# Interaction scratch laid out by quad, x loaded by quad, the last stores dealt out anew

## What is computed

```python
combined = concatenate([dense[:, None, :], e], axis=1)              # (2048, 27, 128)
interactions = einsum('bfd,bgd->bfg', combined, combined)           # (2048, 27, 27)
z = concatenate([dense, interactions[:, iu, ju]], axis=1)           # iu, ju: f < g
h = relu(concatenate([z, dense], axis=1) @ W_top1 + b_top1)         # (2048, 512)
h = relu(h @ W_top2 + b_top2)                                       # (2048, 256)
y = h @ W_top3                                                      # (2048, 1)
```

## Time and profile before

| | |
|---|---|
| runs | 359.15, 359.31, 359.65 us |
| profiled execution | 359.83 us |
| its span | 358.0 us |
| TensorE products busy | 325.9 us |
| VectorE busy | 240.7 us |
| ACT busy | 183.7 us |
| GpSimd busy | 250.0 us |
| mean granted clock of TensorE | 0.986 |
| DMA packets under 512 B | 26790 of 48069 |

### The profile page before, as it was taken

One profiled execution on the slowest core, in us unless ns is written; L12 is line 12 of the kernel. 1 busy time (PEld: TensorE's weight loads), 2 busy tenths in 40 slices (PEclk: granted clock), 3 DMA queues, 4 the chain that ended last, 5 costly groups with the idle time before them and its releaser, 6 DMA issues.

```text
span 358.0 us, 10391 instructions
## 1 busy us (share of the span) xinstructions
PE 325.9 (91%) x4192; PEld 312.3 (87%) x4192; DVE 240.7 (67%) x721; ACT 183.7 (51%) x360; POOL 250.0 (70%) x264
## 2 busy tenths in 40 slices
PE   0558789999999999999999999999999999999576
PEld 0548679989999998999899999999899999998565
DVE  3889987996469762995389654986299556951012
ACT  1345555556633763457534664557445664366224
POOL 5777777777777777777777777777777777775020
PEclk9987999999999999999999999999999999999989
DMA  5999657664447434662457444653356344421230
GB/s 146 235 249 246 157 160 193 158 168 133 99 101 181 115 76 103 139 170 69 99 120 187 95 82 106 149 149 69 103 131 185 82 98 102 125 68 46 34 78 0
DMA packets 48069, 44.80 MB, mean 125 GB/s; under 512 B 26790, under 2 KB 42150, under 8 KB 48022
## 3 DMA queue, kind: packets, MB, share of 16 engines
q1 hardware_dynamic: 38448, 26.89, 31.8%
q0 software_dynamic: 8320, 16.87, 19.5%
q10 hardware_dynamic: 1254, 0.39, 0.6%
HBM read 39.33 MB, written 4.78 MB: 123 GB/s over the span
## 4 chain that ended last, share of the span: by engine, by line
PE 81%; DVE 7%; DMA 6%; SPq 2%; ACT 2%; issue 1%; POOL 0%; ACTq 0%
PE ps_o L335 39%; PE ps_m L386 16%; PE ps_g L375 15%; PE ps_t L346 7%; DVE onehot L749 5%; DMA oh_ids<-onehot_ids 3%; DVE tbl_lo L734 2%; DMA interaction_scratch<-inter 2%; PE ps_m L416 2%; SPq L207 1%; DMA x<-interaction_scratch 1%; PE ps_g L446 1%; POOL interaction_scratch L190 0%; SPq L228 0%; ACT emb L555 0%
## 5 line engine op out<-in xcount | busy, mean ns | idle before, releaser
L313 POOL DMA_INDIRECT rows<-tables,idx x256 | 247.4, 966 | 80.4 <-issue 76.9
L749 DVE TENSOR_SCALAR onehot<-oh_ids,rownum 125x256 fp32r<-125x256 int32 x640 | 200.2, 388 | 50.9 <-PE ps_o L335 43.1
L335 PE MATMUL ps_o<-onehot,tbl_hi 125*128 125x256 f32 x640 | 163.9, 295 | 22.0 <-DVE tbl_lo L734 21.8
L335 PE MATMUL ps_o<-onehot,tbl_lo 125*128 125x256 f32 x640 | 159.0, 287 | 0.0
L335 PEld LDWEIGHTS ps_o<-onehot,tbl_hi 125*128 125x128 f32 x640 | 125.0, 195 | 27.3 <-DVE tbl_lo L734 23.3
L335 PEld LDWEIGHTS ps_o<-onehot,tbl_lo 125*128 125x128 f32 x640 | 125.4, 196 | 0.0
L555 ACT ACTIVATE emb<-ps_o 128x256 f32<-128x256 f32 x80 | 49.3, 740 | 87.0 <-PE ps_o L335 87.0
L375 PEld LDWEIGHTS ps_g<-emb 128*54 128x54 f32 x2048 | 53.6, 130 | 4.8 <-issue 1.8
L375 PE MATMUL ps_g<-emb 128*54 128x54 f32 x2048 | 56.0, 214 | 1.8 <-ACT emb L581 0.8
L571 ACT ACTIVATE emb<-ps_t 128x512 f32<-128x512 f32 x63 | 45.8, 729 | 9.9 <-PE ps_t L346 9.6
L595 ACT ACTIVATE inter<-ps_g 128x432 f32<-128x432 f32 x64 | 33.9, 532 | 15.6 <-PE ps_g L375 13.1
(11 more groups left out here) (60 smaller groups left out, 206.5 us busy)
## 6 DMA issues: line engine op xcount, KB each, us to landing
oh_ids<-onehot_ids SPq DMA_DIRECT2D x80, 128.0 KB
rows<-tables,idx POOLq DMA_INDIRECT x256, 2.4
x<-interaction_scratch SPq DMA_DIRECT2D x23, 117.0 KB
inter<-small_tables SPq DMA_DIRECT2D x4, 448.0 KB
interaction_scratch<-inter SPq DMA_DIRECT2D x30, 47.2 KB
x<-small_tables SPq DMA_DIRECT2D x3, 448.0 KB
h<-small_tables SPq DMA_DIRECT2D x3, 448.0 KB
interaction_scratch<-inter SPq DMA_DIRECT2D x32, 38.2 KB
```

The lines of the kernel that those rows point to most:

```text
L313: pool.indirect_dma_start(rows[e][:, k, :], None, tables[k], bass.IndirectOffsetOnAxis(ap=idx[:, NG * hh + k:NG * hh + k + 1], axis=0),).t ...
L335: mm = pe.matmul(o, tbl[p][:, k, c, :], onehot[n % SLOTS_OH][:, c, :], start=(c + p == 0), stop=(c == TCHUNKS - 1 and p == 1))
L749: op = nc.vector.tensor_scalar(onehot[n % SLOTS_OH][:, c, :], oh_ids[0:TPART, n % IDS, :], rownum[:, c:c + 1], None, ALU.is_equal)
```

## The change

The scratch gets the quad as its outermost dimension, so its order is (quad, f, g, 64 examples), and stores and loads follow. A row that a store writes is now one run in DRAM and one run in SBUF. `load_x` loads a chunk quad by quad, four DMAs of 117 rows of 64 examples, and `split_x_hi` waits for all four. In the last block SP issues quads 0 and 1 of bands 0 and 1 and of the wrapped part, then quads 0 and 1 of x's chunk 0, and all quads of chunks 1 and 2; ACT issues quads 2 and 3 of bands 0 and 1, of the wrapped part and, after its relus, of chunk 0. GpSimd's stores of band 2 no longer wait for band 0.

```diff
@@ build_tower
-    scratch = nc.dram_tensor("interaction_scratch", (FEATURES, WRAP, QUAD, TB), f32,
+    scratch = nc.dram_tensor("interaction_scratch", (QUAD, FEATURES, WRAP, TB), f32,
                              kind="Internal").ap()
@@ store_band
-                eng.dma_start(scratch[f0:f1, f0 + 1:g1, q, :],
+                eng.dma_start(scratch[q, f0:f1, f0 + 1:g1, :],
                               inter[p + f0:p + f1, col + f0 + 1:col + g1, :]).then_inc(stored, 16)
@@ store_wrapped
-                eng.dma_start(scratch[f0:FEATURES, FEATURES:WRAP, q, :],
+                eng.dma_start(scratch[q, f0:FEATURES, FEATURES:WRAP, :],
                               inter[p + f0:p + FEATURES, col:col + SHIFTS, :]).then_inc(inter_stored[WRAPPED], 16)
@@ load_x
-        def load_x(eng, i, c):
+        def load_x(eng, i, c, quads):
...
-            src = bass.AP(tensor=scratch.tensor, offset=(PAIR_F * c * (WRAP + 1) + 1) * BLOCK,
-                          ap=[[BLOCK, SHIFTS], [(WRAP + 1) * BLOCK, PAIR_F], [1, BLOCK]])
-            eng.dma_start(x[0:PAIR_ROWS, c, :], src).then_inc(x_loaded[c], 16)
+            for q in quads:
+                src = bass.AP(tensor=scratch.tensor, offset=((q * FEATURES + PAIR_F * c) * WRAP + PAIR_F * c + 1) * TB,
+                              ap=[[TB, SHIFTS], [(WRAP + 1) * TB, PAIR_F], [1, TB]])
+                eng.dma_start(x[0:PAIR_ROWS, c, TB * q:TB * (q + 1)], src).then_inc(x_loaded[c], 16)
@@ sync, turn_interactions
-                    load_x(sp, i, c)
+                    load_x(sp, i, c, range(QUAD))
@@ sync, the last block
-            store_band(sp, LAST, 0, range(0, 2), inter_stored[0])
-            store_band(sp, LAST, 1, range(QUAD), inter_stored[1])
+            for b in range(2):
+                store_band(sp, LAST, b, range(0, 2), inter_stored[b])
+            store_wrapped(sp, LAST, range(0, 2))
+            load_x(sp, LAST, 0, range(0, 2))
             for c in range(1, PAIR_CHUNKS):
-                load_x(sp, LAST, c)
+                load_x(sp, LAST, c, range(QUAD))
@@ gpsimd
-            pool.wait_ge(inter_stored[0], 16 * QUAD * BLOCKS)
             store_band(pool, LAST, 2, range(QUAD), last_stored)
@@ scalar, split_x_hi
-                    act.wait_ge(x_loaded[c], 16 * (m + 1))
+                    act.wait_ge(x_loaded[c], 16 * (m + 1) * (1 if c == PAIR_CHUNKS else QUAD))
@@ scalar, last_body
-                store_band(act, LAST, 0, range(2, QUAD), inter_stored[0])
-                store_wrapped(act, LAST, range(QUAD))
+                for b in range(2):
+                    store_band(act, LAST, b, range(2, QUAD), inter_stored[b])
+                store_wrapped(act, LAST, range(2, QUAD))
                 relus2(m)
-                load_x(act, LAST, 0)
+                load_x(act, LAST, 0, range(2, QUAD))
                 copy_y(m)
```

## The result

The changed kernel takes 363.70 us (median, 362.31 to 365.80), the kernel before 359.41 beside it: a ratio of 1.0129, 95% interval 1.0083 to 1.0175. The forecast was 359.7 us, no change, with a range to 362.3: the kernel is slower, and by more than that range allows. Ratios come from all timed executions of both kernels but a few far above the rest (one of e_fill_before2 took 532.59 us), so they can differ a little from the quotient of the medians. The profiled execution took 364.32 us with a span of 362.5, against 359.83 and 358.0.

The account below looks back on a forecast made before the run. TensorE was the bound up to 336 us, then a chain of stores, loads and splits. Tail +0.1 and first block +0.25 took the profiled 359.83 to 360.2 us; being 0.5 above the median, forecast 359.7, range 357.4 to 362.3.

Parts of the forecast that it names:

- rival A: SP's queue: quad loads are cheaper to issue than a whole chunk, below 0.70 us each; 356.2 to 357.7 us, chance 0.25.
- B's price: SP's queue: quad loads become dearer, from 0.81 us each on; at 0.93 the kernel takes 362.4 us, chance 0.18.
- D: Stores and loads: the rows aren't joined and the stores stay as they are; about 365 us, chance 0.05.
- part 3: The tail after the last Gram copy: chunk 2's split starts at 348.6 instead of 348.50, +0.1 us.
- so this wait hides: Last block: wrapped stores land at 340.2, chunk 1's first load is due at 340.1, so waiting for them costs nothing.
- rival C: Tail: TensorE's clock falls before chunk 2, +1.4 us for it and up to 2 for layer 2; 361 to 363, chance 0.12.
- Part 4: The body: SP's longer loads stay hidden except in the first block, where TensorE waits 0 to 0.7 us, +0.25 us.

Follow-up runs that it names:

- e_fill_before2: The kernel before with 28 products that nobody reads before layer 3 of block 6; median 358.56 us, ratio 0.9970 to the kernel before.
- e_layout_only: The changed kernel's new layout and quad loads, with the last block's stores dealt out as before; median 362.69 us, ratio 1.0106 to the kernel before.
- e_no_band1: The changed kernel without the last block's stores of band 1, its loads untouched; 361.15 us in one run.
- e_pool_c2: The changed kernel with the last block's four loads of chunk 2 on GpSimd's queue instead of SP's; 362.97 us, ratio 1.0101 to the kernel before.
- e_last_fill: e_last_only with unread products before layer 3 of block 6 and before the last block's three chunks; 361.32 us, ratio 1.0049 to the kernel before.
- e_last_only: The kernel before with new layout, quad loads and new dealing in the last block alone; median 364.23 us, ratio 1.0124 to the kernel before.
- e_body_act: The kernel before with only blocks 0 to 6 changed, ACT issuing the first block's four loads of chunk 2; 359.43 us, ratio 0.9999.
- e_fill_after: The changed kernel with unread products before layer 3 of block 6 and before the last block's three chunks; 363.87 us, ratio 1.0124 to the kernel before.
- e_first_act: The changed kernel with the first block's four loads of chunk 2 issued by ACT instead of SP; 364.30 us, ratio 1.0149 to the kernel before.
- after_again: The changed kernel once more, unedited, on another chip; median 365.33 us, ratio 1.0142 to the kernel before.

## Why the prediction was wrong

**Right.** The stores were joined. A quad load costs 0.77 us of SP's queue (forecast 0.79), so rival A is dead and B's price wasn't reached; D is refuted. GpSimd left the end chain. TensorE waits for x only once in the body. Chunk 2's split is released by its load behind a serial queue. The two signs by which I would have called myself wrong, GpSimd in the end chain and a TensorE wait for x in a later block, didn't appear; neither looks at the landings. The Trainium skill (DMA: Bandwidth & Descriptors, Rules for kernel authors) says to join small transfers, as under 64 KB one pays mostly overhead. The trace agrees: the twelve loads of a block of the body hold SP's queue for 10.28 us, where three held it for 2.93.

**Wrong, part 3: "so this wait hides".** Each term from the first store's start (forecast, then measured):

| step | forecast | measured |
|---|---|---|
| chunk 0's first load | +2.65 | 339.94 - 336.35 = +3.59 |
| last wrapped store issued | +2.25 | +2.53 |
| its landing | 2.2 | 3.81 |
| chunk 1's first load | +4.35 | 342.75 - 336.35 = +6.40 |
| seven gaps between loads | 5.85 | 5.77 |
| from the last load's start to the split | 2.6 | 2.30 |
| split of chunk 2 | +12.85 | +14.47 |

More than the whole miss of 1.6 us stands in the fourth line (2.05 us late; the two lines before the last give 0.4 back), and most of it is the landing: I took 2.2 us, the least of the landings of GpSimd's stores in the earlier trace rows, and it was 3.81. With 3.8 the same sum gives +6.05 for chunk 1 and says "wait". The serial loads, which I had as the bound from 338.4 on, became the bound only behind that wait. That the issues of two queues beside each other cost more (six of SP's in 3.14 us, 0.52 each, not 0.395) is the smaller part.

That the new 3.81 equals the 3.81 of the earlier trace rows is chance. The old one is ACT's second store of band 0, and that store now lands after 2.94 us (337.00 to 339.94), as joined rows had been expected to help. The row that answers to the last wrapped store wasn't among mine. In the trace of before it was issued at 340.06, and the load that waited for it started at 343.10, 3.0 us later:

```profile
340.06 0.59 ACTq L199 DMA_DIRECT2D interaction_scratch<-inter  x1
...
343.10 0.83 SPq L219 DMA_DIRECT2D x<-interaction_scratch  x1
```

With 3.0 the sum gives +5.25, a wait of 0.9 us and a little under half the miss. Most of the rest goes with the new dealing: 2.93 us in e_layout_only, which has the new layout and the old dealing, against 3.69 to 4.61 in the seven traces with both. GpSimd's four stores, which now fly beside the others, are the nearest candidate; no run brings back GpSimd's wait alone in the changed kernel, so this stays open.

e_no_band1 moved the split by the 1.1 us of the wait, e_pool_c2 by 2.8 when the serial queue was shortened, e_last_fill priced the step at 1.8 us of time.

Part 3 also said that TensorE's chunks 0 and 1 "all come earlier". They came later: their splits start 8.65 and 11.20 us after the last Gram copy, before 8.22 and 10.21. Before, TensorE ran from layer 3 through chunk 1 without a pause; now it waits ahead of each chunk, and that is where rival C comes in.

**Wrong, rival C.** The mechanism was named, with a chance of 0.12 and "no row shows a fall after one so short". By the mean clocks it happened in every timed execution of e_last_only, where it cost 2.7 us (forecast 1.4 to 3.4), more than the later split. The reasoning failed in taking the 4.5 us of one row as needed: the fall came behind idle times of 1.02, 0.85 and 1.61 us in the changed kernel and of 0.94 and 1.51 us in e_last_only. It didn't come behind 1.85 and 1.49 us in e_layout_only, so the length of an idle time doesn't foretell it. The later landings of part 3 made these pauses.

**Part 4: right mechanism, undersized.** Forecast 0.25 us. The twelfth load started at 79.8 (forecast 79.3) and the split was done at 82.99 (82.8); but TensorE, whose layer began at 80.84, was due at its tenth product at 81.92, 0.8 us before the 82.74 of the forecast, and waited 0.97. In other executions the wait was 0.9 to 2.6, and twice a fall of the clock came on top. Body alone: 0.39%, or 0.9 us by the medians. That moving four loads removes it (e_body_act) speaks for place and cause. One execution's phase was read as fixed.

**Open.** e_fill_after should be near 1.0088 by the parts (0.49% + 0.39%) and is 1.0124; e_first_act should be near e_last_only's 1.0124 and is 1.0149, no gain from a repair that works in e_body_act. Both gaps lie within the summed intervals, so they don't refute the account, but neither repair is shown to help the changed kernel itself.

## What to carry to other kernels

Where transfers are on the critical path, sum what one queue issues serially and the landing of what each issue waits for. Take the landing from the row of the same store, never the least of a range, and try the sum with 1 us more where the change puts more stores in the air at once. Where TensorE works in bursts at the end of a kernel, look at its granted clock: here an edit that moved the last split by some 2 us cost 4.8 by the medians (e_last_only), and 43 idle products took it back to 1.8 (e_last_fill). Such products are a cheap trial. A split of one DMA into four multiplies the price of the queue by four, and is free only where that queue has the time in its tightest block, not in the typical one.

## What the runs showed of the hardware

- The issue of a load of 117 rows cost 0.77 us at 256 B per row and 0.79 at 1024 B; the issue of a store of 9 rows of up to 5.4 KB 0.315 at the median.
- From issue to landing, ACT's last wrapped store of the last block took 3.0 us in pieces of 256 B; in joined rows 2.93 with the old dealing and 3.69 to 4.61 with the new. ACT's second store of band 0 took 3.81 in pieces and 2.94 joined; GpSimd's took 2.2 to 3.3 in pieces and 2.4 to 3.6 joined.
- The granted clock fell to 0.50 behind idle times of 0.85 to 1.61 us (the changed kernel), and in the body behind one of 2.19 (after_again); it didn't fall behind 1.85 and 1.49 in e_layout_only.
- GpSimd's 256 gathers, one about each 1.25 us, run almost without pause from 3.2 to 326.7 us: a second floor close beneath TensorE's. In four executions, two of them with the body of before (e_last_only, e_fill_before2), TensorE waited for them near the end, 0.3 to 1.3 us:

```profile
L316 POOL DMA_INDIRECT rows<-tables,idx x256: 940/944/1962, 3.2 to 326.7; - x128
```

```profile
PE ps_t L347 <- DMA rows<-tables,idx: 1.3, 1, 1.3
```

The first line is from the changed kernel, the second, a wait of TensorE for the gathers, from e_first_act.
